# First layer of a graph network: normalizing the node rows in the edge stage instead of the perceptron stage

## The chip, the cores and the metric

The kernel runs on one core of one Trainium2 chip. The metric is the device time of the whole program in microseconds (us). Three runs of the kernel before took 6508.22, 6519.34 and 6523.56 us, so its median is 6519.34 us. Beside them there is one execution under the hardware profiler.

The engines are PE (TensorE, the matrix engine, with PEld for its weight loads), DVE (VectorE), ACT (ScalarE), POOL (GpSimd) and SP (SyncE, which issues plain DMAs here). POOL issues the indirect DMAs, gathers and scatters of rows.

## What is computed

Four layers over a graph of 50,000 nodes (padded to 50,176) and 25,000 edges (padded to 25,088), rows of 128 floats. Only the first layer is touched by the change:

```python
h = jnp.maximum(_layernorm(x, axis=-1), 0.0)
x = x + _L0_gnn_ref(h, edge_attr_128, W1, b1, W2, b2, gamma, beta, src, dst)

def _L0_gnn_ref(node_feats, edge_feats, W1, b1, W2, b2, gamma, beta, src, dst):
    msg = jax.nn.relu(node_feats[src] + edge_feats)
    agg = jax.ops.segment_sum(msg, dst, num_segments=n_nodes)
    h = node_feats + agg
    h = jax.nn.relu(h @ W1.T + b1) @ W2.T + b2
    mean = jnp.mean(h, axis=0)
    var = jnp.var(h, axis=0)
    return (h - mean) * jax.lax.rsqrt(var + BN_EPS) * gamma + beta
```

Layer normalization is over the 128 features of a row. The normalized rows h are needed in two places: for the 25,000 gathered source rows of the edges, and for all 50,000 nodes. The edges are sorted by destination.

## The kernel before

The program is a chain of stages (`prepare_indices`, `gine_edges`, `gine_mlp`, `gine_finish`, then two graph convolutions, an attention layer and a mean aggregation). A stage is a `Phase`: it allocates its tiles and semaphores, and at its end all engines meet at a barrier and POOL clears the stage's semaphores one by one (line 52). Inside a stage each engine has its own program, written out by hand; engines wait on semaphores. A tile is 512 rows: 128 partitions by 4 rows of 128 floats (`SUB` = 4), 256 KB.

`pipeline(eng, bodies, tiles, steps)` (line 228) writes an engine's order: for each turn t it emits every step (lag, function) for tile t - lag, in the order of the list. So the order of the list is the order of the engine's queue, and a step with lag 1 works on the tile before. A loop body holds 7 tiles in the edge stage (`K`) and 14 in the perceptron stage (`NB`), and each tile of a body has its own buffer, 7 of them (`RING`).

**The edge stage** (`gine_edges`, line 313) has 49 tiles of 512 edges, 7 bodies. SP loads the indices, the edge features and the `keep` row of each of the 7 tiles, then fills the table AGG in DRAM with zeros in 14 DMAs of 1792 KB (line 345), then reloads the tiles of the next body as their scatters land (`agg_out`). POOL (line 352) gathers the source rows of x with 4 indirect DMAs per tile (line 157), waits for the zero fill, and then, per body, scatters each tile's sums to AGG with 4 indirect DMAs (line 163); from the fourth tile on a gather of the next body follows each scatter, and the last four gathers of a body stand together. For each tile the other engines run a ring:

- DVE `moments`: statistics (line 186) and moments (line 194) of the gathered rows; ACT `root` (line 199); DVE `scales`: reciprocal (line 208) and shift (line 212); ACT `normalize`: four activations (line 217, the helper `Norm.apply`), which write relu((x - mean) / std) in place.
- DVE `add` (line 407) adds the edge features; PE `turn` transposes the message (line 420); ACT `copy_turned` (line 443) applies relu and copies it out of PSUM.
- DVE `scan` (line 400) sums along the sorted edges, with `keep` as the reset; PE `turn_back` (line 428) transposes back; ACT `copy_back` (line 448) writes `rows`, which POOL scatters.

DVE's list is moments, scan of the tile before, add (with the scales ahead of it). ACT's is root, copy_back of the tile before, normalize, copy_turned.

**The perceptron stage** (`gine_mlp`, line 455) has 98 tiles of 512 nodes. SP loads x and AGG of a tile; DVE takes the statistics of x, ACT the root, DVE reciprocal and shift, ACT normalizes x into `h` (four activations, line 217); POOL adds `agg` (line 511) and issues one small scatter to a table of positions POS (line 163); PE transposes (line 583), multiplies by W1 (line 590) and by W2 (line 596); ACT copies the transposed tile (`sT`, line 615) and makes the hidden layer (`hidT`, line 621); DVE adds the bias (line 538) and takes statistics for the batch normalization (line 543); SP stores YT. All of `gine_finish` reads YT and x and writes the DRAM tables X and H; H is written there for the first time.

## Time and profile before

| | |
|---|---|
| median of 3 runs | 6519.34 us |
| profiled execution, its own time | 6571.89 us |
| its span | 6570.1 us |
| busy, share of the span | PE 55%, PEld 31%, DVE 57%, ACT 39%, POOL 60% |
| granted TensorE clock, mean over the span | 0.767 |
| edge stage | from the barrier at about 29 us to POOL's last scatter, issued at 641.68 us |
| perceptron stage | from 652.7 us to about 993 us |

How to read the rows below. Times are us from the start of the span. In the table of stretches each row is a stretch, its length, the busy time of PE, PEld, DVE, ACT and POOL with the number of instructions in brackets, then the granted TensorE clock (1.00 is full), the busy share of the 16 DMA engines and GB/s. In the order of time each row is start, duration, engine, line, operation, what it writes <- what it reads, shapes, and x with the number of instructions merged into the row; in square brackets stands the time that the engine was idle before it and what released it. "issue" is time without a wait that the profile shows, "remote" a release that it ascribes to none of this core's engines. In the list of waits the columns are: who waited for whom, us in total, times, longest. SPq is SP's queue of DMA issues. A busy engine is not always at work: an instruction held by another one counts as busy.

### The profile page before, as it was taken

The page shows a single profiled execution, that of the slowest core. Times are in us where ns is not written, and L with a number is a line of the kernel's source. Part 1 is how long each engine was busy: PE and PEld are TensorE (multiplying, and loading weights), DVE is VectorE, ACT ScalarE, POOL GpSimd, SP SyncE. Part 2 cuts the span into 40 slices and gives each one's busy share as a digit, 9 for nine tenths or more (in the row PEclk, how much of TensorE's full clock was granted, in tenths as well). Part 3 has the DMA queues.
Part 4 walks back from the last instruction along what each step waited for, and adds up shares of the span by engine and source line. Part 5 has one row for each costly group of instructions (what it writes and reads, how often), then busy time and mean ns, then how long its engine had stood idle before and what let it go on. Part 6 is the DMA issues. An engine that isn't in the chain of part 4 may idle for free. (4 is left out here: it accounts for less than half of the span.)

```text
span 6570.1 us, 69946 instructions
## 1 busy us (share of the span) xinstructions
PE 3610.1 (55%) x13980; PEld 2028.2 (31%) x13980; DVE 3759.2 (57%) x11380; ACT 2554.3 (39%) x5795; POOL 3939.5 (60%) x3763
## 2 busy tenths in 40 slices
PE   1111673368775893454777689444223337995333
PEld 0111332222222453341322245343201115664222
DVE  2222898824345887992443588699635564554323
ACT  1222887724443114662444311577523332332000
POOL 4676667754451457885554145899866615554766
PEclk9999995578887997756898899656556668996555
DMA  7332769811111224541111022666445542333222
GB/s 231 84 87 64 258 227 337 307 42 35 36 37 29 65 67 153 175 152 45 39 40 35 24 72 70 208 233 235 151 125 178 173 142 65 104 103 111 85 79 69
DMA packets 507700, 784.36 MB, mean 119 GB/s; under 512 B 150737, under 2 KB 185144, under 8 KB 505568
## 3 DMA queue, kind: packets, MB, share of 16 engines
q1 hardware_dynamic: 413408, 623.08, 28.5%
q0 software_dynamic: 94080, 159.09, 8.9%
q14 instruction: 156, 1.28, 0.1%
q8 instruction: 56, 0.92, 0.1%
HBM read 476.20 MB, written 316.91 MB: 121 GB/s over the span
## 5 line engine op out<-in xcount | busy, mean ns | idle before, releaser
L913 DVE TENSOR_TENSOR conv_logits_leaky<-conv_logits_z,conv_logits_sloped 128x512 f32<-128x512 f32 x784 | 527.4, 689 | 538.3 <-ACT conv_logits_sloped L876 318.0
L157 POOL DMA_INDIRECT conv_logits_hd<-H,conv_logits_idx x392 | 370.7, 946 | 548.9 <-issue 448.1
L839 PE MATMUL conv_logits_z<-conv_logits_hdT,wsum 128*128 128x512 f32 x784 | 466.7, 733 | 277.8 <-issue 190.5
L876 ACT ACTIVATE conv_logits_sloped<-conv_logits_z 128x512 f32<-128x512 f32 x784 | 453.5, 601 | 401.4 <-remote 115.3
L1317 PE MATMUL conv_nodes_o_ps<-wmean,conv_nodes_hT 128*128 128x128 f32 x1568 | 338.6, 383 | 460.7 <-ACT conv_nodes_hT L1382 402.0
L163 POOL DMA_INDIRECT AGG<-conv_aggregate_rows,conv_aggregate_idx x392 | 381.7, 974 | 313.5 <-ACT conv_aggregate_rows L1159 178.2
L1317 PEld LDWEIGHTS conv_nodes_o_ps<-wmean,conv_nodes_hT 128*128 128x128 f32 x1568 | 289.8, 277 | 527.8 <-ACT conv_nodes_hT L1382 464.8
L157 POOL DMA_INDIRECT conv_logits_hs<-H,conv_logits_idx x392 | 370.7, 946 | 126.6 <-issue 126.6
L847 PE MATMUL conv_logits_z<-diffT,wl 128*128 (+1 forms) x784 | 385.8, 638 | 77.4 <-DVE conv_logits_leaky L913 77.4
L1123 PE MATMUL conv_aggregate_y<-wl,conv_aggregate_diff 128*128 128x512 f32 x784 | 408.3, 654 | 22.7 <-issue 14.3
L217 ACT ACTIVATE conv_nodes_scaled<-conv_nodes_o,conv_nodes_norm_shift,conv_nodes_norm_rstd 128x128 f32<-128x128 f32 x784 | 322.2, 481 | 169.0 <-DVE conv_nodes_norm_shift L212 164.7
L1186 DVE SCALAR_TENSOR_TENSOR conv_aggregate_part<-conv_aggregate_y,conv_aggregate_alpha,conv_aggregate_part 128x128 f32<-128x128 f32 x1176 | 358.4, 346 | 20.6
L839 PEld LDWEIGHTS conv_logits_z<-conv_logits_hdT,wsum 128*128 128x128 f32 x784 | 159.0, 222 | 573.9 <-issue 462.6
L1274 POOL TENSOR_TENSOR conv_nodes_agg<-conv_nodes_agg,conv_nodes_bias 128x512 f32<-128x512 f32 x196 | 248.5, 1268 | 105.8 <-DVE conv_nodes_res L1351 39.3
L157 POOL DMA_INDIRECT gat_aggregate_xd<-X,idx x196 | 185.4, 946 | 208.6 <-DVE gat_aggregate_x L1769 153.8
L903 DVE TENSOR_TENSOR diffT<-conv_logits_hsT_ps,conv_logits_hdT 128x512 f32 (+1 forms) x98 | 67.8, 692 | 397.2 <-ACT conv_logits_hdT L870 217.4
L163 POOL DMA_INDIRECT AGG<-gine_edges_rows,gine_edges_idx x196 | 203.2, 1037 | 151.4 <-issue 107.8
L1520 PE MATMUL gat_logits_e_ps<-gat_logits_hdT,gat_logits_wa 128*4 128x512 f32 x98 | 84.6, 963 | 375.5 <-ACT gat_logits_hdT L1533 176.1
L163 POOL DMA_INDIRECT out<-mean_edges_rows,idx x196 | 210.5, 1074 | 105.0 <-issue 57.3
L157 POOL DMA_INDIRECT gat_logits_hd<-H,idx x196 | 193.1, 985 | 127.7 <-remote 60.3
L1149 ACT ACTIVATE conv_aggregate_alpha<-conv_aggregate_alpha_ps 128x16 f32<-128x16 f32 x98 | 18.0, 184 | 566.2 <-issue 148.9
L157 POOL DMA_INDIRECT gine_edges_hs<-x,gine_edges_idx x196 | 199.1, 1016 | 61.4 <-issue 59.2
(249 smaller groups left out, 10371.5 us busy)
## 6 DMA issues: line engine op xcount, KB each, us to landing
conv_nodes_h<-H SPq DMA_DIRECT2D x196, 256.0 KB, 2.7
conv_nodes_agg<-AGG SPq DMA_DIRECT2D x196, 256.0 KB, 3.0
AGG<-gine_edges_zero SPq DMA_DIRECT2D x14, 1792.0 KB
gine_mlp_x<-x SPq DMA_DIRECT2D x98, 256.0 KB
gine_mlp_agg<-AGG SPq DMA_DIRECT2D x98, 256.0 KB
YT<-gine_mlp_yT SPq DMA_DIRECT2D x98, 256.0 KB
gine_finish_x<-x SPq DMA_DIRECT2D x98, 256.0 KB
gine_finish_yT<-YT SPq DMA_DIRECT2D x98, 256.0 KB
```

Source lines behind the costliest of these rows:

```text
L157: return pool.indirect_dma_start(out=out, out_offset=None, in_=table, in_offset=bass.IndirectOffsetOnAxis(ap=index, axis=0))
L163: return pool.indirect_dma_start(out=table, out_offset=bass.IndirectOffsetOnAxis(ap=index, axis=0), in_=rows, in_offset=None, bounds_check ...
L217: last = act.activation(out[:, a, :], x[:, a, :], func, bias=self.shift[k][:, a:a + 1], scale=self.rstd[k][:, a:a + 1])
L839: pe.matmul(z[h][:, :], g.wsum[:, h * D:(h + 1) * D], hdT[slot(k)][:, :], start=True, stop=True).then_inc(z_done[0], 1)
L847: pe.matmul(z[h][:, :], g.wl[:, h * D:(h + 1) * D], g.diffT[:, bass.ds(n * TILE, TILE)], start=False, stop=True, skip_group_check=True).th ...
L876: act.activation(sloped[H * j + h][:, :], z[h][:, :], ACT.Copy, scale=SLOPE).then_inc(sloped_made[j], 1)
L913: dve.tensor_tensor(leaky[H * j + h][:, :], z[h][:, :], sloped[H * j + h][:, :], ALU.max).then_inc(leaky_made[j], 1)
L1123: pe.matmul(y[s][:, :], diff[slot(k)][:, s * P:(s + 1) * P], g.wl[:, :], start=True, stop=True).then_inc(y_done, 1)
L1186: last = dve.scalar_tensor_tensor(out=out, in0=yh, scalar=a, in1=out, op0=ALU.mult, op1=ALU.add)
L1274: pool.tensor_tensor(flat(agg[r]), flat(agg[r]), bias[:, :], ALU.add).then_inc(agg_made, 1)
L1317: last = pe.matmul(o_ps[k % 2][:, a, :], hT[k % 2][:, a * P:(a + 1) * P], g.wmean[:, :], start=True, stop=True)
L1520: pe.matmul(e_ps[n % 2][:, :], wa[:, 1, :], hdT[n % 2][:, :], start=True, stop=False)
```

## The change

In the edge stage two tiles of nodes are now handled beside each tile of edges (49 x 2 = 98). SP loads their x rows and later stores the normalized rows to H; DVE and ACT do the normalizing, with steps of their own in their lists (`node_scales` and `node_normalize` one tile behind). The perceptron stage loads H in the place of x, has no normalizing left, and POOL's addition waits for the load itself. The lags of its lists shrink with the steps that are gone.

```diff
@@ gine_edges
+        x, h = ([m.sbs(f"{n}{c}_", [P, SUB, D]) for c in range(2)] for n in ("x", "h"))
+        node_norm = [Norm(m, f"node_norm{c}") for c in range(2)]
+        x_in, h_out = ([m.sems(f"{n}{c}_") for c in range(2)] for n in ("x_in", "h_out"))
+        node_made = [m.sem(f"node_made{c}") for c in range(2)]
...
+                def load_nodes(k, i):
+                    for c in range(2):
+                        sp.dma_start(x[c][k][:, :, :], node_rows(g.x, (i * K + k) * 2 + c)).then_inc(x_in[c][k], 16)
+                def store_nodes(k, i):
+                    for c in range(2):
+                        sp.wait_ge(node_made[c], i * K + k + 1)
+                        sp.dma_start(node_rows(g.H, (i * K + k) * 2 + c), h[c][k][:, :, :]).then_inc(h_out[c][k], 16)
                 for k in range(K):
                     load(k, 0)
+                for k in range(K):
+                    load_nodes(k, 0)
                 sp.wait_ge(zero_set, 1)
...
                         for k in range(K):
+                            store_nodes(k, i - 1)
+                            load_nodes(k, i)
                             sp.wait_ge(agg_out[k], i * 64 + agg0)
                             load(k, i)
+                for k in range(K):
+                    store_nodes(k, nb - 1)
...
+                def node_moments(k, i):
+                    for c in range(2):
+                        dve.wait_ge(x_in[c][k], i * 16 + 16)
+                        node_norm[c].take_stats(dve, x[c][k], k)
+                    for c in range(2):
+                        node_norm[c].moments(dve, k, i * K + k + 1)
+                def node_scales(k, i):
+                    for c in range(2):
+                        node_norm[c].invert(dve, k, i * K + k + 1)
+                    for c in range(2):
+                        node_norm[c].shifts(dve, k, i * K + k + 1)
-                pipeline(dve, nb, K, [(0, moments), (1, scan), (0, add)])
+                pipeline(dve, nb, K, [(0, moments), (1, scan), (1, node_scales), (0, node_moments), (0, add)])
...
+                def node_normalize(k, i):
+                    for c in range(2):
+                        act.wait_ge(node_norm[c].shift_done, i * K + k + 1)
+                        past(act, h_out[c][k], i * 16)
+                        node_norm[c].apply(act, h[c][k], x[c][k], k, ACT.Relu).then_inc(node_made[c], 1)
+                def node_root(k, i):
+                    for c in range(2):
+                        node_norm[c].root(act, k, i * K + k + 1, eps)
                 pipeline(act, nb, K, [
                     (0, lambda k, i: norm.root(act, k, i * K + k + 1, eps)),
-                    (1, copy_back), (0, normalize), (0, copy_turned)])
+                    (1, copy_back), (0, normalize), (1, node_normalize), (0, node_root), (0, copy_turned)])
@@ gine_mlp
-                    sp.dma_start(x[r][:, :, :], node_rows(g.x, n)).then_inc(tile_in[r], 16)
+                    sp.dma_start(h[r][:, :, :], node_rows(g.H, n)).then_inc(tile_in[r], 16)
...
-                node_stream(sp, nb, load, freed, store, 5)
+                node_stream(sp, nb, load, freed, store, 4)
...
-                    pool.wait_ge(h_made, n + 1)
+                    wait_alone(pool, tile_in[r], 32 * (turns(k, i) + 1), steps_own)
...
-                pipeline(dve, nb, NB, [
-                    (0, take_stats),
-                    (9, copy_y),
-                    (1, lambda k, i: norm.moments(dve, k % RING, i * NB + k + 1)),
-                    (3, lambda k, i: norm.scales(dve, k % RING, i * NB + k + 1)),
-                    (9, measure_y)])
+                pipeline(dve, nb, NB, [(6, copy_y), (6, measure_y)])
...
-                pipeline(act, nb, NB, [
-                    (0, lambda k, i: norm.root(act, k % RING, i * NB + k + 1, eps)),
-                    (2, normalize), (4, copy_turned), (6, hidden)])
+                pipeline(act, nb, NB, [(0, copy_turned), (2, hidden)])
```

Where the instructions stand now, at two places. First ACT in the loop of the edge stage, one tile, before (`norm_std` is the root, `rows` the copy back, `hs` the normalized gathered rows, `msgT` the copy of the turned message):

```order
L199 ACTIVATE gine_edges_norm_std<-gine_edges_norm_mv,gine_edges_eps 128x4 [waits gine_edges_norm_mv_done]
L448 ACTIVATE gine_edges_rows<-gine_edges_back 128x512 [waits scattered2,gine_edges_back_psum]
L217 ACTIVATE gine_edges_hs<-gine_edges_hs,gine_edges_norm_shift,gine_edges_norm_rstd 128x128 [waits gine_edges_norm_shift_done]
L217 ACTIVATE gine_edges_hs<-gine_edges_hs,gine_edges_norm_shift,gine_edges_norm_rstd 128x128 x3
L443 ACTIVATE gine_edges_msgT<-gine_edges_turned 128x512 [waits gine_edges_msgT_psum]
```

The same place after the change:

```order
L199 ACTIVATE gine_edges_norm_std<-gine_edges_norm_mv,gine_edges_eps 128x4 [waits gine_edges_norm_mv_done]
L483 ACTIVATE gine_edges_rows<-gine_edges_back 128x512 [waits scattered3,gine_edges_back_psum]
L217 ACTIVATE gine_edges_hs<-gine_edges_hs,gine_edges_norm_shift,gine_edges_norm_rstd 128x128 [waits gine_edges_norm_shift_done]
L217 ACTIVATE gine_edges_hs<-gine_edges_hs,gine_edges_norm_shift,gine_edges_norm_rstd 128x128 x3
L217 ACTIVATE gine_edges_h_3<-gine_edges_x_3,gine_edges_node_norm_shift,gine_edges_node_norm_rstd 128x128 [waits gine_edges_h_out0_3,gine_edges_node_norm0_shift_done]
L217 ACTIVATE gine_edges_h_3<-gine_edges_x_3,gine_edges_node_norm_shift,gine_edges_node_norm_rstd 128x128 x3
L217 ACTIVATE gine_edges_h_3<-gine_edges_x_3,gine_edges_node_norm_shift,gine_edges_node_norm_rstd 128x128 [waits gine_edges_h_out1_3,gine_edges_node_norm1_shift_done]
L217 ACTIVATE gine_edges_h_3<-gine_edges_x_3,gine_edges_node_norm_shift,gine_edges_node_norm_rstd 128x128 x3
L199 ACTIVATE gine_edges_node_norm_std<-gine_edges_node_norm_mv,gine_edges_eps 128x4 [waits gine_edges_node_norm0_mv_done]
L199 ACTIVATE gine_edges_node_norm_std<-gine_edges_node_norm_mv,gine_edges_eps 128x4 [waits gine_edges_node_norm1_mv_done]
L478 ACTIVATE gine_edges_msgT<-gine_edges_turned 128x512 [waits gine_edges_msgT_psum]
```

Eight activations and two roots now stand between the normalizing of a tile and the copy of its turned message. Second, DVE in the edge stage from the scan to the addition, after the change (before it, the reciprocal of the edge rows followed the scan at once):

```order
L422 SCALAR_TENSOR_TENSOR gine_edges_sumT<-gine_edges_keep,gine_edges_sumT,gine_edges_msgT 128x512 [waits gine_edges_scanned,gine_edges_msgT_made]
L208 RECIPROCAL gine_edges_node_norm_rstd<-gine_edges_node_norm_std 128x4 [waits gine_edges_node_norm0_std_done]
L208 RECIPROCAL gine_edges_node_norm_rstd<-gine_edges_node_norm_std 128x4 [waits gine_edges_node_norm1_std_done]
L212 SCALAR_TENSOR_TENSOR gine_edges_node_norm_shift<-gine_edges_node_norm_mv,gine_edges_node_norm_rstd 128x4 [waits gine_edges_node_norm0_rstd_done]
L212 SCALAR_TENSOR_TENSOR gine_edges_node_norm_shift<-gine_edges_node_norm_mv,gine_edges_node_norm_rstd 128x4 [waits gine_edges_node_norm1_rstd_done]
L186 BN_STATS gine_edges_node_norm_stats<-gine_edges_x_5 128x6 [waits gine_edges_x_in0_5]
L186 BN_STATS gine_edges_node_norm_stats<-gine_edges_x_5 128x6 x3
L186 BN_STATS gine_edges_node_norm_stats<-gine_edges_x_5 128x6 [waits gine_edges_x_in1_5]
L186 BN_STATS gine_edges_node_norm_stats<-gine_edges_x_5 128x6 x3
L194 BN_AGGR gine_edges_node_norm_mv<-gine_edges_node_norm_stats 128x2 [waits gine_edges_node_norm0_stats_done]
...
L208 RECIPROCAL gine_edges_norm_rstd<-gine_edges_norm_std 128x4 [waits gine_edges_norm_std_done]
L212 SCALAR_TENSOR_TENSOR gine_edges_norm_shift<-gine_edges_norm_mv,gine_edges_norm_rstd 128x4 [waits gine_edges_norm_rstd_done]
```

The scales of the last two node tiles and the statistics and moments of the next two stand ahead of the two small instructions that ACT's normalizing of the gathered rows waits for.

## Rows read from the trace of the kernel before

**Rows 1.** Table of stretches: the zero fill, the rest of the edge stage, the perceptron stage.

```profile
29.00:110.00 81.00, 14.46 (x52) 9.29 (x52) 24.44 (x86) 21.40 (x49) 28.16 (x29) 1.00 0.98 385
109.60:642.60 533.00, 94.75 (x340) 60.79 (x340) 142.88 (x505) 124.45 (x295) 374.40 (x364) 1.00 0.29 82
700.00:800.00 100.00, 76.97 (x256) 34.15 (x256) 98.94 (x379) 91.46 (x223) 71.35 (x64) 1.00 0.77 251
```

**Rows 2.** Order of time, edge stage: POOL's DMAs beside DVE's statistics and beside the scan.

```profile
256.59 0.95 POOL L157 DMA_INDIRECT gine_edges_hs<-x,gine_edges_idx  x1 [0.30 <-issue]
256.82 0.87 DVE L186 BATCH_NORM_STATS2 gine_edges_norm_stats<-gine_edges_hs 128x6 f32<-128x128 f32 x4 [5.10 <-issue]
306.05 1.36 POOL L163 DMA_INDIRECT AGG<-gine_edges_rows,gine_edges_idx  x1 [0.30 <-issue]
```

**Rows 3.** List of waits, 115 to 640 us.

```profile
ACT gine_edges_rows L448 <- remote: 89.8, 10, 10.5
ACT gine_edges_msgT L443 <- remote: 88.1, 11, 9.2
POOL AGG L163 <- ACT gine_edges_rows L448: 43.6, 7, 9.5
```

**Rows 4.** Order of time, edge stage: the ring of one tile, DVE and ACT.

```profile
302.81 0.69 DVE L407 TENSOR_TENSOR gine_edges_msg<-gine_edges_hs,gine_edges_ea 128x512 f32<-128x512 f32 x1 [9.79 <-ACT gine_edges_hs L217]
...
304.44 0.38 DVE L194 BATCH_NORM_AGGREGATE gine_edges_norm_mv<-gine_edges_norm_stats 128x2 f32<-128x6 f32 x4 [0.15 <-DVE gine_edges_norm_stats L186]
304.71 0.60 ACT L443 ACTIVATE gine_edges_msgT<-gine_edges_turned 128x512 f32<-128x512 f32 x1 [1.93 <-issue]
...
305.34 1.28 DVE L400 TENSOR_TENSOR_SCAN gine_edges_sumT<-gine_edges_keep,gine_edges_sumT,gine_edges_msgT 128x512 f32<-128x512 f32 x1 [0.53 <-issue]
306.54 0.15 DVE L208 RECIPROCAL gine_edges_norm_rstd<-gine_edges_norm_std 128x4 f32<-128x4 f32 x1
...
308.32 1.64 ACT L217 ACTIVATE gine_edges_hs<-gine_edges_hs,gine_edges_norm_shift,gine_edges_norm_rstd 128x128 f32<-128x128 f32 x4
...
309.99 0.69 DVE L407 TENSOR_TENSOR gine_edges_msg<-gine_edges_hs,gine_edges_ea 128x512 f32<-128x512 f32 x1 [3.10 <-ACT gine_edges_hs L217]
```

**Rows 5.** Order of time, edge stage: a shift and the scatter beside it.

```profile
149.45 0.97 POOL L163 DMA_INDIRECT AGG<-gine_edges_rows,gine_edges_idx  x1 [0.30 <-issue]
149.54 0.16 DVE L212 SCALAR_TENSOR_TENSOR gine_edges_norm_shift<-gine_edges_norm_mv,gine_edges_norm_rstd 128x4 f32<-128x4 f32 x1
```

**Rows 6.** Order of time, perceptron stage: the ring of one tile.

```profile
803.56 1.26 POOL L511 TENSOR_TENSOR gine_mlp_s<-gine_mlp_h,gine_mlp_agg 128x512 f32<-128x512 f32 x1 [0.78 <-ACT gine_mlp_h L217]
804.05 0.78 DVE L212 SCALAR_TENSOR_TENSOR gine_mlp_norm_shift<-gine_mlp_norm_mv,gine_mlp_norm_rstd 128x4 f32<-128x4 f32 x1
804.95 1.65 ACT L217 ACTIVATE gine_mlp_h<-gine_mlp_x,gine_mlp_norm_shift,gine_mlp_norm_rstd 128x128 f32<-128x128 f32 x4 [0.30 <-DVE gine_mlp_norm_shift L212]
806.50 0.57 ACT L615 ACTIVATE gine_mlp_sT<-gine_mlp_turned 128x512 f32<-128x512 f32 x1
806.74 1.26 POOL L511 TENSOR_TENSOR gine_mlp_s<-gine_mlp_h,gine_mlp_agg 128x512 f32<-128x512 f32 x1 [0.79 <-ACT gine_mlp_h L217]
```

**Rows 7.** Order of time: the second and the last of POOL's 98 additions.

```profile
677.70 1.27 POOL L511 TENSOR_TENSOR gine_mlp_s<-gine_mlp_h,gine_mlp_agg 128x512 f32<-128x512 f32 x1
...
976.49 1.27 POOL L511 TENSOR_TENSOR gine_mlp_s<-gine_mlp_h,gine_mlp_agg 128x512 f32<-128x512 f32 x1 [0.71 <-ACT gine_mlp_h L217]
```

**Rows 8.** Order of time: PE while the perceptron stage drains.

```profile
978.41 0.60 PE L583 MATMUL gine_mlp_turned<-gine_mlp_ident,gine_mlp_s 128*128 128x128 f32 x4
...
981.24 0.60 PE L583 MATMUL gine_mlp_turned<-gine_mlp_ident,gine_mlp_s 128*128 128x128 f32 x4
```

**Rows 9.** Order of time: POOL's first instruction after the barrier between the stages.

```profile
652.74 0.21 POOL L168 MEMSET gine_mlp_ident<- 128x128 f32 x1 [10.09 <-POOLq L52]
```

**Rows 10.** Order of time, edge stage: two neighbouring issues of SP in a late stretch.

```profile
366.22 0.70 SPq L339 DMA_DIRECT2D gine_edges_keep<-KEEP  x1
371.15 0.73 SPq L337 DMA_DIRECT2D gine_edges_idx<-IDX  x1
```

More of the change, by code:

```diff
@@ L464, in gine_mlp @@
         gamma, beta, eps = m.sb("gamma", [D, 1]), m.sb("beta", [D, 1]), m.sb("eps", [P, 1])
-        x, agg, h, s = (m.sbs(n, [P, SUB, D]) for n in ("x", "agg", "h", "s"))
+        agg, h, s = (m.sbs(n, [P, SUB, D]) for n in ("agg", "h", "s"))
         sT, hidT, yT = m.sbs("sT", [P, TILE]), m.sbs("hidT", [P, TILE]), m.sbs("yT", [P, TILE])
@@ L603, in _ @@
                 act.wait_ge(weights_in, 6 * 16)
-                def normalize(k, i):
-                    r, n = k % RING, i * NB + k
-                    act.wait_ge(norm.shift_done, n + 1)
-                    past(act, s_made, n + 1 - RING)
-                    norm.apply(act, h[r], x[r], r, ACT.Relu).then_inc(h_made, 1)
                 def copy_turned(k, i):
```

12 lines of the change are left out of this document (5 added, 7 removed).

## The prediction

> **What bounds the kernel now.** I read the table of stretches first, to find the two stages that the diff touches. The edge stage (29 to 643 us) has two parts. While AGG is filled with zeros the 16 DMA engines are busy 0.98 of the time at 385 GB/s, and no scatter may start [rows 1]. From 109.6 to 642.6 us it is a different picture: DMA 0.29, DVE 142.88 us and ACT 124.45 us of 533, and POOL 374.40 us in 364 indirect DMAs, 1.029 us each [rows 1]. Each of these has 0.30 us of issue ahead of it [rows 2], so POOL's queue wants 364 x 1.33 = 484 us; 49 us of idle time are left, 43.6 of them in 7 waits for the rows that ACT copies out [rows 3]. So **POOL's descriptor queue bounds the edge stage**, at 8 x 1.33 = 10.6 us a tile.
>
> Then the order of time, for the ring that feeds POOL: DVE adds, PE transposes ("turns"), ACT copies, DVE scans, PE turns back, ACT copies, ACT normalizes the next tile, DVE adds again. From add to add it takes 309.99 - 302.81 = 7.18 us [rows 4]. It has 3.4 us a tile to spare against POOL.
>
> In the perceptron stage DVE looks full (98.94 of 100 us) at a TensorE clock granted at 1.00, the 2.4 GHz level [rows 1]. It is not full of work: the shift of 128x4, 0.16 us elsewhere [rows 5], lasts 0.78 us and ends when POOL's addition ends [rows 6]. The ring is ACT's four normalizing activations (1.65 us), POOL's addition (1.26 us), DVE's shift, ACT again: 806.74 - 803.56 = 3.18 us [rows 6]. From the second addition to the last it is (976.49 - 677.70) / 96 = 3.11 us a tile [rows 7].
>
> **The change, part by part.**
>
> *Perceptron stage.* Statistics, roots, scales and normalizing go, 16 small instructions and their waits per tile. The loads stay two per tile (H in the place of x), so SP and DMA have what they had. POOL's addition waits for the load alone. What is late next: when the stage drains, ACT has no normalizing left and one tile takes 981.24 - 978.41 = 2.83 us, in the ring turn, copy, hidden copy, second product, turn [rows 8]. The order of these on PE and ACT is as before. That is the row I take. 96 tiles x (3.11 - 2.83) = **-27 us**. The bounds: nothing at all (0), or POOL's own pace. POOL's part of a tile is 1.26 + 0.16 + about 1.0 = 2.45 us, so (3.11 - 2.45) x 96 = -63. DMA is no bound: 3 x 262 KB a tile is 2.0 us at the 385 GB/s of the zero fill [rows 1]. The start is unchanged: after its first addition POOL waits for the store of POS.
>
> *Fourteen loads ahead of the zero fill.* They are 14 x 262 KB = 3.67 MB put into a queue that is the bound there; at 385 GB/s that is 9.5 us, and at the bandwidth of the fill's own part a little less. Everything from the first scatter moves by it: **+9 us** (bounds 0, if the loads slip into DMA's free beginnings, and 12).
>
> *The ring of the edge stage.* Per tile DVE gets 8 + 8 statistics instructions and 4 small ones, ACT 8 activations and 2 roots; POOL and PE get nothing. In the new order ACT does the node activations between normalize and the copy of the turned tile, and DVE does the node work between scan and add; both lie in the ring. From the end of normalize: 8 activations at 1.55 us per four, which is the distance from one group's start to the next instruction [rows 6], 3.1; two roots 0.5; copy to scan 0.63; scan to reciprocal 1.20; four small DVE instructions 0.7; statistics and moments of two tiles, each 0.87 and 0.38 [rows 2, 4] less 0.08 where one group starts into the other, 2 x 1.09 + 0.1 = 2.3; reciprocal, shift and hand-over 0.45; normalize and hand-over 1.67 [rows 4]. The sum is 10.5 us. The turns of PE and the copy back lie beside this. So the ring goes from 7.2 to 10.5 us and stands **level with POOL's 10.6**: in the middle of the stage it costs nothing, but the spare time is gone. It shows at the end, where POOL has only scatters left (4 x 1.33 = 5.3 us a tile) and the ring brings a tile each 10.5: two tiles late, 2 x 5.2 = **+10 us**. Bounds: 0, if the ring is still ahead by then; and if each added ACT instruction took its full busy time (8 x 0.48 + 2 x 0.29) with 0.3 more of waits, 11.4 us a tile, 49 x 0.8 = 39.
>
> *SP and DMA in the edge stage.* Four DMAs more per tile. SP waits for the node rows of tile k before it loads the next body's x, indices and edge rows of tile k; ACT makes these rows one tile behind, as it does the rows that the scatter waits for, so SP's wait for the scatter still comes last. 4 x 262 KB per 10.6 us are 99 GB/s beside 82 GB/s, far from 385. I take 0 (bounds 0 and 10). H's store waits only for itself, 7 tiles later.
>
> *Semaphores.* The edge stage clears 42 more and the next one 7 fewer. POOL's 10.09 us between the stages [rows 9] hold 34 clears beside a landing and a barrier, so 35 more are under 10; I take **+2**.
>
> *What VectorE's new work does to POOL.* A scatter beside the scan lasts 1.36 us instead of 0.97. A gather beside statistics lasts 0.95 and a scatter beside a 128x4 shift 0.97, nothing more [rows 2, 5]. So the added DVE work costs POOL 0. The Trainium skill, page SBUF — State Buffer, section on the two separate sides, says that a DVE instruction with two SBUF inputs and a GpSimd one that reads SBUF exclude each other through a shared port pair, for the whole instruction. The long scan agrees; by the rule the two added shifts of a tile would block too, 98 x 0.16 = 16 us more, and the sum would be 6529. The row of the shift speaks against it.
>
> The sum is -27 + 9 + 10 + 2 = **-6 us**, against the profiled execution (span 6570.1, itself 6571.9 us). That execution lies 52.6 us above the median 6519.34; I carry the difference over to the median, since no term scales with it: 6519 - 6 = **6513 us**.
>
> **The rivals.**
>
> *Rival 1, the ring passes its delays on (slower).* In some stretches ACT's copies start late although PE is done: 21 waits of 8.5 us in the mean, put down to no engine [rows 3], where about 2 us is normal [rows 4]. That is 21 x 6.5 = 137 us of delay, and 49 us of it reached POOL; the 3.4 us of spare time took the rest. Without spare time more reaches POOL. The copy of the turned tile is covered by 3.6 us of node work, so 2.9 of its 6.5 would show, 11 times: 32. The copy back shows about 5, 10 times: 50 to 65. With what lengthens the ring a little beyond POOL (0.3 a tile, 15), 97 to 112 in place of 49, so +48 to +63 on the sum; if only half the stretches come, +24. The middle of these ends is about +41, and with the sum's own -6 the time is 6519 + 35 = 6554. It decides from a ring longer than 10.6 us. Against it: the 52.6 us between the profiled execution and the median are as large as POOL's 49 us of idle time, so an execution without the profiler may hardly have these delays; then there is nothing to pass on.
>
> *Rival 2, all of the new work hides (faster).* The ring keeps ahead, the fill takes the loads for 3, and the perceptron stage goes at 2.7 instead of 2.83: -39 + 3 + 2 = -34, 6485. For it: DVE and ACT are idle for three quarters of the edge stage. Against it: PE and ACT keep their order, and the drained rows show it [rows 8].
>
> *Rival 3, SP falls behind.* SP issues 7 DMAs per tile instead of 3, in order, behind two new waits. In a late stretch two issues in a row stand 371.15 - 366.22 = 4.93 us apart [rows 10]; if all issues of one tile in three took half of that, 2.5, these tiles would need 17.5 us of SP against POOL's 10.6, and POOL would wait for its indices: 7 us on 16 tiles less what the lead of three tiles takes, some +90, 6603. Against it: SP now waits for scatters, not for its own issues.
>
> **How the numbers follow.** A measurement of this kernel tells 0.2%, 13 us, from no change: below 6506 is faster, above 6532 slower. The forecast has 0.47, with a range of its own of 6497 to 6527: it falls 0.12 faster, 0.32 same and 0.03 slower. Rival 1 has 0.33, of it 0.06 same and 0.27 slower. Rival 2 has 0.14, faster. Rival 3 has 0.06, slower. That makes 0.26 faster, 0.38 same, 0.36 slower. The range that leaves out the outer halves of rivals 2 and 3 and the tail of rival 1 is 6486 to 6575.
>
> **What would show it.** Right: the first scatter at about 118 us instead of 109.6; add to add in the edge stage 10 to 11 us everywhere, no longer 7.2; POOL's last scatter some 20 us later than 642; one perceptron tile in 2.83 us, and DVE half idle there, with no shift of 0.78 us left. Wrong: an add-to-add distance over 11.5 us, with POOL waiting for the copied rows for more than 70 us (rival 1); a perceptron tile still over 3 us or at 2.5; POOL waiting for its indices (rival 3); gathers longer than 1.0 us beside statistics.

## The result and the profile after

The changed kernel takes **6604.21 us** (median of 4 runs, 6591.32 to 6620.54), the kernel before 6520.73 us (4 runs, 6508.22 to 6523.56). The ratio is 1.0135, with a 95% interval of 1.0114 to 1.0155: slower by 83.5 us. The forecast was 6513 with a range up to 6575, and its likeliest case was wrong; the sign and the mechanism are those of rival 1, at about twice its price.

The profiled execution of the changed kernel took 6620.54 us (span 6618.7). First its table of stretches, zero fill, rest of the edge stage and 100 us of the perceptron stage, which answers to [rows 1]:

```profile
29.00:120.00 91.00, 13.35 (x48) 8.58 (x48) 40.99 (x222) 38.69 (x101) 27.12 (x29) 1.00 1.00 395
119.90:758.00 638.10, 95.82 (x344) 61.46 (x344) 254.14 (x1350) 276.46 (x734) 363.61 (x364) 1.00 0.46 141
810.00:910.00 100.00, 84.74 (x281) 37.37 (x280) 50.40 (x71) 41.11 (x71) 91.44 (x82) 1.00 0.88 282
```

POOL does the same 364 DMAs in 363.61 us, but the stretch is 638 us long in the place of 533. The perceptron stage is no longer full of DVE (50.40 for 98.94). Where the 105 us went is in the list of waits, 115 to 760 us, answering to [rows 3]:

```profile
ACT gine_edges_hs L217 <- DVE gine_edges_norm_shift L212: 183.3, 37, 17.0
POOL AGG L163 <- ACT gine_edges_rows L483: 149.7, 18, 13.9
...
DVE gine_edges_node_norm_mv L194 <- remote: 52.0, 19, 4.1
...
PE gine_edges_back L463 <- remote: 39.6, 5, 9.0
DVE gine_edges_norm_shift L212 <- remote: 28.9, 8, 8.2
ACT gine_edges_norm_std L199 <- remote: 27.6, 8, 7.0
DVE ne_edges_node_norm_shift L212 <- remote: 15.6, 6, 4.9
DVE gine_edges_norm_mv L194 <- remote: 12.5, 4, 5.6
```

POOL waits 149.7 us for copied rows, 106 more than before (43.6). The late releases ("remote"), before on ACT's two copies alone, now sit on DVE, PE and ACT's root, the new instructions among them. Order of time, edge stage; first two additions of an undisturbed part, then pieces of one tile in a late stretch:

```profile
314.96 0.69 DVE L429 TENSOR_TENSOR gine_edges_msg<-gine_edges_hs,gine_edges_ea 128x512 f32<-128x512 f32 x1 [1.72 <-ACT gine_edges_hs L217]
...
324.58 0.69 DVE L429 TENSOR_TENSOR gine_edges_msg<-gine_edges_hs,gine_edges_ea 128x512 f32<-128x512 f32 x1 [1.72 <-ACT gine_edges_hs L217]
```

```profile
207.72 0.69 DVE L429 TENSOR_TENSOR gine_edges_msg<-gine_edges_hs,gine_edges_ea 128x512 f32<-128x512 f32 x1 [2.89 <-ACT gine_edges_hs L217]
...
216.58 0.30 ACT L199 ACTIVATE gine_edges_norm_std<-gine_edges_norm_mv,gine_edges_eps 128x4 f32<-128x4 f32 x1 [4.95 <-issue]
...
219.39 0.16 DVE L212 SCALAR_TENSOR_TENSOR ne_edges_node_norm_shift<-gine_edges_node_norm_mv,ine_edges_node_norm_rstd 128x4 f32<-128x4 f32 x1 [5.93 <-issue]
...
234.48 1.65 ACT L217 ACTIVATE gine_edges_hs<-gine_edges_hs,gine_edges_norm_shift,gine_edges_norm_rstd 128x128 f32<-128x128 f32 x4 [14.74 <-DVE gine_edges_norm_shift L212]
...
236.16 0.69 DVE L429 TENSOR_TENSOR gine_edges_msg<-gine_edges_hs,gine_edges_ea 128x512 f32<-128x512 f32 x1 [1.71 <-ACT gine_edges_hs L217]
...
244.09 1.00 POOL L163 DMA_INDIRECT AGG<-gine_edges_rows,gine_edges_idx  x1 [13.43 <-ACT gine_edges_rows L483]
```

Undisturbed, a tile takes 9.62 us from add to add, 1 us less than POOL's 10.6 (in place of 7.18 in [rows 4]). The disturbed one takes 236.16 - 207.72 = 28.4 us: a root stands 4.95 us and a shift 5.93 us, both put down to "issue", and so on, each behind the other. POOL then stands 13.43 us.

At the end of the stage, where POOL only scatters, it waits for the ring at each of the last five tiles. The first of these waits lies behind a late stretch; the last four are 4.8 us each, 19.3 us together:

```profile
714.25 0.97 POOL L163 DMA_INDIRECT AGG<-gine_edges_rows,gine_edges_idx  x1 [13.87 <-ACT gine_edges_rows L483]
...
723.89 0.97 POOL L163 DMA_INDIRECT AGG<-gine_edges_rows,gine_edges_idx  x1 [4.84 <-ACT gine_edges_rows L483]
...
752.75 0.97 POOL L163 DMA_INDIRECT AGG<-gine_edges_rows,gine_edges_idx  x1 [4.82 <-ACT gine_edges_rows L483]
```

Two rows of the perceptron stage, 2.83 us apart (3.18 in [rows 6]), and the first instruction behind the barrier, answering to [rows 9]:

```profile
901.14 1.26 POOL L555 TENSOR_TENSOR gine_mlp_s<-gine_mlp_h,gine_mlp_agg 128x512 f32<-128x512 f32 x1 [0.33 <-issue]
...
903.97 1.26 POOL L555 TENSOR_TENSOR gine_mlp_s<-gine_mlp_h,gine_mlp_agg 128x512 f32<-128x512 f32 x1 [0.43 <-issue]
```

```profile
770.34 0.21 POOL L168 MEMSET gine_mlp_ident<- 128x128 f32 x1 [12.78 <-POOLq L52]
```

By stages, after less before: first scatter 119.97 for 109.59, +10.4; first to last scatter 636.6 for 532.1, **+104.5**; from there to the next stage +2.7; perceptron stage (from its identity fill to that of `gine_finish`) 316.7 for 344.1, **-27.4**. The sum is +90.2, and the medians without the profiler differ by 83.5. So the loss of the edge stage is no product of profiling. The two profiled executions as a whole differ by 48.6 us only: the rest of the program, which the change does not touch, took 5573 us in the one before and 5532 in this one. Most of the 52.6 us by which the profiled execution of the kernel before lay above its median would then stand behind the two stages; a second profiled execution of it, to compare with, there is not.

### The profile page after: what moved, and what is told of

It is laid out like the page before. It is cut to its first block and busy times, and to the rows that moved or that the text cites. A ratio compares the mean times of both kernels' runs of the same rounds, so it can differ in the third digit from the quotient of the medians.

```text
span 6618.7 us, 70480 instructions
## 1 busy us (share of the span) xinstructions
PE 3605.0 (54%) x13980; PEld 2023.8 (31%) x13980; DVE 3719.3 (56%) x11380; ACT 2556.7 (39%) x5795; POOL 3936.2 (59%) x3763
## 5 line engine op out<-in xcount | busy, mean ns | idle before, releaser
L163 POOL DMA_INDIRECT AGG<-gine_edges_rows,gine_edges_idx x196 | 196.1, 1000 | 259.7 <-ACT gine_edges_rows L483 149.7
L455 PE MATMUL gine_edges_turned<-gine_edges_ident,gine_edges_msg 128*128 128x128 f32 x196 | 54.6, 434 | 413.8 <-DVE gine_edges_msg L429 226.6
```

Source lines behind the costliest of these rows:

```text
L163: return pool.indirect_dma_start(out=table, out_offset=bass.IndirectOffsetOnAxis(ap=index, axis=0), in_=rows, in_offset=None, bounds_check ...
```

## The experiments

They ran on four chips, and the kernel before was timed beside each set: B 5732.1 us (e1 to e4), C 5731.9 (f1 to f4), D 6538 and 6540 (g1 to g3, h1 to h5), E 6497 (j1). So there are two kinds of chip for this kernel, the slower taking 13 to 14% more. The result's chip, A, is like D and E; its number was not noted, so it may be one of them. Each chip was used in one or two sittings, so what differs may also be something that goes along with the chip. This difference turned out to be the best experiment of the study. Ratios are to the kernel before on the same chip. The kernel before was traced on A alone, and the changed kernel was timed on A and C alone.

**The parts alone, chip B.** e1 has the new `gine_edges` with the old `gine_mlp`. e2 is the other way round:

```diff
 gine_mlp, e2 (gine_edges as before)
-   sp.dma_start(h[r][:, :, :], node_rows(g.H, n)).then_inc(tile_in[r], 16)
+   sp.dma_start(h[r][:, :, :], node_rows(g.x, n)).then_inc(tile_in[r], 16)
```

> Edge stage of the changed kernel, perceptron stage of the kernel before (it normalizes its rows itself; what the edge stage stored is overwritten later and read by nobody in between). Every theory in which the perceptron stage gained 27 us expects 6631 us (6604 + 27), 110 us over the kernel before. If the perceptron stage gained little without the profiler, the time is that of the changed kernel, 6604.

Measured: 5742.13 us, ratio **1.0016** (1.0006 to 1.0027). A miss for every theory: the edge part costs 9 us here and not 110. (By the traces the next stage begins 19.7 us later in e1 than in e2, 623.6 for 603.9; with no trace of the kernel before on this chip the 10 us between the two figures stay open.)

> Edge stage of the kernel before, perceptron stage of the changed kernel; it adds the plain node rows in place of the normalized ones, which leaves out the first normalization of the node rows. The traces give the perceptron stage 316.7 us for 344.1: 6493 us, 27 under the kernel before. It is the base that the two next runs are compared with. A gain under 10 us would say that the stage is bound by something else without the profiler.

Measured: 5694.19 us, **0.9937** (0.9923 to 0.9950), -36 us. By the traces of e1 and e2 the stage is 344.7 and 316.1 us long, -28.6; the 7 us between the two figures are open too.

e3 keeps the transfers and drops the work (its stores write one constant tile, so the normalization is left out); e4 keeps the work and drops the transfers (the perceptron stage adds plain rows):

```diff
 e3
-   sp.wait_ge(node_made[c], i * K + k + 1)
-   sp.dma_start(node_rows(g.H, ...), h[c][k][:, :, :])
+   sp.wait_ge(x_in[c][k], i * 16 + 16)
+   sp.dma_start(node_rows(g.H, ...), h[0][0][:, :, :])
-   (1, scan), (1, node_scales), (0, node_moments), (0, add)
+   (1, scan), (0, add)
-   (0, normalize), (1, node_normalize), (0, node_root), (0, copy_turned)
+   (0, normalize), (0, copy_turned)
 e4
-   store_nodes(k, i - 1)
-   load_nodes(k, i)
-   dve.wait_ge(x_in[c][k], i * 16 + 16)
+   dve.wait_ge(x_in[c][k], 16)
-   gine_mlp: node_rows(g.H, n)
+   gine_mlp: node_rows(g.x, n)
```

> The changed kernel without its work on the node rows in the edge stage: all loads of x and all stores into H are there, seven issues of SP to a tile, but VectorE and ScalarE do nothing with them (the stores write one constant tile, so the normalization is left out and the sums are of other numbers). Theory A, the work in the ring of an edge tile takes the spare time and lets delays through to POOL: 6493 + 9 (loads ahead of the zero fill) = 6502, 6495 to 6515. Theory B, the transfers and SP's issues in order slow the gathers and scatters: 6604 or nearly, at least 6570. Theory C, each is harmless alone and only the sum of them costs: under 6520 here and under 6520 in the next run.

Measured: 5722.10 us, 0.9984 (0.9975 to 0.9993).

> The changed kernel with its work on the node rows, but without the transfers: the fourteen tiles of x are loaded once and normalized again in every body, nothing is stored, and the perceptron stage adds plain node rows (so its output lacks the first normalization). Theory A: 6604 less at most 10, so 6590 to 6604, with POOL waiting some 150 us for copied rows as in the changed kernel. Theory B: about 6502. Theory C: under 6520.

Measured: 5700.30 us, 0.9944 (0.9930 to 0.9958). Both are under the kernel before, which is what theory C says, but nothing was there to be told apart: the whole loss was missing on this chip. The traces say why. No wait of the edge stage in e1 to e4 is put down to "remote", and POOL waits for copied rows for at most 1.2 us in each of the four.

**The changed kernel elsewhere, and delays by hand, chip C.** The delays, in the kernel before (f2) and in the changed one (f3):

```diff
 copy_turned
     act.wait_ge(msgT_psum, i * K + k + 1)
+    if k in (1, 3, 5):
+        for d in range(3):
+            past(act, pad_made, i * 9 + k // 2 * 3 + d)
+            act.activation(pad[:, :], zero[:, :], ACT.Copy).then_inc(pad_made, 1)
```

> The changed kernel itself, once more. Where the kernel before takes some 5730 us, as in the four runs above, the parts add up to 5732 + 9 (edge part, e1) - 38 (perceptron part, e2) = 5703, a ratio of 0.995, with POOL waiting under 5 us for copied rows in the edge stage. Where it takes some 6520 us, 1.0135 with 140 us of such waits. If the result of 1.0135 has a cause beside those waits, the ratio is over 1.000 here although they are missing.

Measured: 5712.41 us, ratio **0.9963** (0.9950 to 0.9977): the same program that loses 1.35% on chip A gains 0.4% here. Its table of stretches from the first scatter to the last, and DVE's additions (count, shortest, median and longest ns, first and last start):

```profile
119.00:607.00 488.00, 94.70 (x340) 60.73 (x340) 245.24 (x1349) 273.54 (x723) 376.70 (x364) 1.00 0.59 185
```

```profile
L429 DVE TENSOR_TENSOR gine_edges_msg<-gine_edges_hs,gine_edges_ea x42: 691/692/693, 154.9 to 590.3; 128x512 f32<-128x512 f32 x42
```

The stretch that took 638 us on chip A takes 488, with the same work and the same granted clock of 1.00, and the ring goes at POOL's pace: (590.3 - 154.9) / 41 = 10.6 us a tile.

> The kernel before with delays put in by hand: in tiles 1, 3 and 5 of each body of seven, ScalarE fills a buffer three times (estimate 9 us, from 597 ns for a 512 wide copy) between its wait for the turned messages and their copy, 21 delays in the stage. Theory A (a delay of the ring reaches POOL only as far as the tiles between have no spare time): the ring takes 7.2 us, POOL 10.6, so 2.33 tiles give back 7.9 us of each 9: 21 x 1.1 = 23 us over the kernel before, 10 to 60. Theory B (what a delay costs does not hang on the spare time, for the gathered tiles ahead absorb it or nothing does): 0, or 21 x 9 = 189 us.

Measured: 5760.38 us, 1.0057 (1.0043 to 1.0070), +28.5 us. One fill took 3.19 us, so a delay was 9.6 us. In the trace DVE's additions stand 7.2 to 7.5 us apart where there is no delay between them and 16.8 where there is one (9.5 to 9.8 and 19.2 in f3). POOL's waits for copied rows in f2, and behind them those of f3:

```profile
POOL AGG L163 <- ACT gine_edges_rows L454: 40.7, 11, 12.0
```

> The changed kernel with the same delays. Theory A: its ring takes 9.6 us, so 2.33 tiles give back 2.3 us of each 9: 21 x 6.7 = 141 us over the changed kernel, and some 90 us over the kernel before with the same delays (141 - 23 - 29), which would be the sign and the size of the result. Theory B: the same addition as in the kernel before.

Measured: 5840.83 us, 1.0196 (1.0182 to 1.0210), +128.4 us over f1 and **+80.5 over f2**.

```profile
POOL AGG L163 <- ACT gine_edges_rows L489: 141.9, 14, 14.4
```

21 delays by hand bring on this chip what chip A does by itself: 40.7 and 141.9 us of waits for 43.6 and 149.7, and 80 us between the kernels for 83.5. Number and length of the delays are near those of the late copies on A (21 of 8.5 us in the mean), so that the sizes agree is in part by design. What the two runs decide is that the same delays cost 28.5 us beside one ring and 128.4 beside the other: theory B, the same addition in both, falls.

f4 is f3 with one more edit, the edge tile's scales taken out of `add` into a step of their own:

```diff
-   (1, scan), (1, node_scales), (0, node_moments), (0, add)
+   (1, scan), (0, scales), (1, node_scales), (0, node_moments), (0, add)
```

> The changed kernel with the same delays and one edit: VectorE makes the scales of the edge tile right behind the scan, ahead of its work on the node rows, which then lies beside ScalarE's normalization of the edge tile. Theory A: the ring falls to some 8 us (7.18 and what ScalarE's 3.2 us of node rows stand over the 2.4 us of addition and turn), 2.33 tiles give back 6.0 of 9: 21 x 3 = 63 us over the changed kernel, some 78 us under the run before this one. If the order of the work does not matter (the busy time of the engines decides, which is the same), it is equal to the run before this one.

Measured: 5802.01 us, 1.0127 (1.0111 to 1.0142), 39 us under f3; the waits for copied rows are 95.9 us. The direction is right and the size half of the expected: the order decides, at equal busy times, but the ring takes 8.6 us from add to add where there is no delay, and not the 8 that I had reckoned.

**The same order without delays, chip D.** g1 is the changed kernel with f4's order. g2 also moves the fourteen first loads behind the zero fill and the node work three tiles back:

```diff
-   for k in range(K):
-       load_nodes(k, 0)
     sp.wait_ge(zero_set, 1)
...
+   for k in range(K):
+       load_nodes(k, 0)
-   DVE (1, node_scales), (0, node_moments)       ACT (1, node_normalize), (0, node_root)
+   DVE (4, node_scales), (3, node_moments)       ACT (4, node_normalize), (3, node_root)
```

> The changed kernel with VectorE's scales of the edge tile right behind the scan, no delays put in. Where the kernel before takes some 5730 us POOL is the bound in both and the time is the changed kernel's, ratio 0.996 (5705 to 5717). Where it takes some 6520 us, theory A gives 6604 less what the shorter ring takes up: with delays put in it was 39 us, so 6565, ratio 1.007; the theory that the ring's spare time does not decide there gives 6604.

Measured: 6580.45 us, ratio **1.0080** (1.0057 to 1.0104), as theory A has it (1.007); the 1.0135 that it is set against is from chip A. POOL's waits:

```profile
POOL AGG L163 <- ACT gine_edges_rows L485: 79.1, 13, 10.6
...
POOL gine_edges_hs L157 <- DMA gine_edges_idx<-IDX: 25.4, 4, 10.6
```

> The same with the fourteen first loads of x behind the zero fill, and with the work on the node rows three tiles later in the lists of VectorE and ScalarE, so that no edge tile waits for them. If the loads ahead of the zero fill cost the 9 to 10 us by which the first scatter moved, this kernel is 9 us under the one above, less what the three node tiles behind the last edge tile add at the end (3 x 3.2 us of ScalarE beside POOL's last scatters, 0 to 10 us): ratio to the kernel before 0.994 to 0.996. If the zero fill is not what the first scatter waits for, equal to the one above or slower by up to 10.

Measured: 6578.67 us, 1.0071 (1.0044 to 1.0098), no gain over g1 that can be told. Its first scatter starts at 109.1 us (118.6 in g1), so the loads ahead of the fill do cost 9.5 us there. The gain is lost at the other end: from the last scatter to the next stage it takes 23.2 us, 13.7 in g1, for the node rows now end three tiles behind (the last scatter is issued at 705.30 us, and ACT normalizes until 720.92). In between one wait took the place of another. POOL in the edge stage of g2 waits for nobody's rows, but 114.6 us for indices, where g1 has 79.1 and 25.4:

```profile
POOL gine_edges_hs L157 <- DMA gine_edges_idx<-IDX: 114.6, 19, 17.1
```

And SP's queue in a late stretch of it, where the x2 rows are two neighbouring issues:

```profile
311.53 0.70 SPq L341 DMA_DIRECT2D gine_edges_idx<-IDX  x1
315.04 0.70 SPq L342 DMA_DIRECT2D gine_edges_ea<-ea  x1
319.23 0.70 SPq L343 DMA_DIRECT2D gine_edges_keep<-KEEP  x1
325.53 4.90 SPq L352 DMA_DIRECT2D H<-gine_edges_h  x2
333.27 3.49 SPq L347 DMA_DIRECT2D gine_edges_x<-x  x2
337.50 0.31 SPq L341 DMA_DIRECT2D gine_edges_idx<-IDX  x1
338.01 0.38 SPq L342 DMA_DIRECT2D gine_edges_ea<-ea  x1
```

From one load of indices to the next SP takes 337.50 - 311.53 = 26 us; behind that it issues three loads in 1.1 us (the third, `keep`, at 338.57). This is rival 3, at work here, where the ring holds nothing up.

> The one above with the 21 delays put in. The node rows lie on the same places of the ring as in the run with the other order and delays (5802 us), so theory A gives that time less 0 to 9 us. If instead the first body profits (its seven tiles run without node work until the zero fill is through, and POOL does not wait for them), it is some 15 us under it.

Measured: 6687.16 us, 1.0229 (1.0198 to 1.0259), on chip D. The number to compare it with was from chip C, so the expectation can't be judged. Over g2, on the same chip, the delays cost 108.5 us.

**Work or transfers, on a chip that has the lateness (D).** h1 and h2 are e3 and e4 again.

> The kernel of e3 (loads of x and stores into H, no work of VectorE and ScalarE on the node rows; the normalization is left out) once more, for a chip on which the kernel before takes some 6520 us. Theory A (the work in the ring costs): before - 27 + 9, ratio 0.996 to 0.999, with some 44 us of waits of POOL for copied rows. Theory B (SP's seven issues a tile cost): 1.010 or more, with POOL waiting for indices. On a chip with the kernel before at 5730 us: 0.998 as in e3.

Measured: 6532.16 us, ratio **0.9991** (0.9967 to 1.0014). POOL and ACT:

```profile
ACT gine_edges_rows L485 <- remote: 77.1, 10, 10.5
POOL gine_edges_hs L157 <- DMA gine_edges_idx<-IDX: 52.8, 9, 10.1
```

> The kernel of e4 (the work on the node rows in the ring, no transfers for it in the loop; the perceptron stage adds plain rows) once more, for the same reason. Where the kernel before takes 6520 us theory A gives 1.011 to 1.0135 with some 130 to 150 us of waits of POOL for copied rows, theory B 0.996. Where it takes 5730 us: 0.994 as in e4.

Measured: 6645.25 us, ratio **1.0157** (1.0131 to 1.0182), somewhat over what I expected, and so are the waits for rows.

```profile
POOL AGG L163 <- ACT gine_edges_rows L476: 164.6, 20, 17.6
...
DVE ne_edges_node_norm_shift L212 <- remote: 32.0, 11, 6.3
```

The work in the ring brings a loss as large as that of the changed kernel, with SP at three loads a tile as before; the transfers alone bring little of it. SP's delays are there in h1: POOL waits 52.8 us for indices, and the 44 us of waits for rows that I expected are gone. One stands in the place of the other.

h4 lets POOL pause, in the changed kernel:

```diff
     for k in range(K):
...
+        if k in (2, 5):
+            wait_alone(pool, pad_made, i * 2 + k // 3, own)
+            pool.memset(pad[:, :], 0.0).then_inc(pad_made, 1)
         if more and k >= BEHIND:
```

> The changed kernel, with POOL filling a 128x3584 buffer (estimate 5.5 us, from 0.206 us for 128x128) before its gathers of tiles 2 and 5 of each body, so that it issues no transfer for that time, 14 times in all. If the late stretches end when POOL issues nothing for 5 us, the late waits in the trace (of PE, ScalarE, VectorE on engines that were done) fall to under a third of the changed kernel's 230 us, and the 77 us of fills are paid back by POOL's 150 us of waits for copied rows: ratio to the kernel before 1.000 to 1.010. If the pauses change nothing in them: the waits for rows still shrink by what the pauses cover, and the late waits stay, ratio 1.0135 to 1.020. Where the kernel before takes 5730 us, there are no late stretches and the pauses cost their own 77 us less POOL's spare: ratio 1.005 to 1.010.

Measured: 6619.68 us, 1.0126 (1.0099 to 1.0153). The late waits:

```profile
PE gine_edges_back L467 <- remote: 63.4, 9, 9.9
DVE ne_edges_node_norm_shift L212 <- remote: 51.4, 16, 6.7
ACT gine_edges_norm_std L199 <- remote: 44.4, 11, 6.5
DVE gine_edges_norm_shift L212 <- remote: 36.1, 9, 9.6
DVE gine_edges_node_norm_mv L194 <- remote: 33.4, 14, 4.0
DVE gine_edges_norm_mv L194 <- remote: 8.0, 2, 4.7
```

237 us, where the same sum over the changed kernel's list is 176 us (on chip A). They did not fall to a third. The time lies between the two forecast ranges and tells nothing by itself. But the fills were shorter than my estimate of 5.5 us:

```profile
L392 POOL MEMSET gine_edges_pad<- x14: 3108/3114/3127, 134.0 to 734.5; 128x3584 f32 x14
```

With pauses of 3.1 us the run doesn't answer what happens when POOL issues nothing for 5 us. The trace of the changed kernel has longer stops of POOL, nine of them of 10 us and more, and there the late stretches do end. It has 48 waits of 1 us and more put down to "remote" on DVE, ACT and PE; 12 of them end inside a stop of over 2.5 us, none later than 5.4 us after its beginning. Of SP's single issues of 0.7 us none starts later than 2.5 us into a stop, while 39 quick ones start later than 4 us into one. The stop of 13.43 us begins when the first of these transfers has ended, at 230.66:

```profile
229.72 0.94 POOL L157 DMA_INDIRECT gine_edges_hs<-x,gine_edges_idx  x1 [0.30 <-issue]
231.24 2.80 SPq L347 DMA_DIRECT2D gine_edges_x<-x  x2
234.08 0.33 SPq L341 DMA_DIRECT2D gine_edges_idx<-IDX  x1
```

So on a chip with late stretches they go along with POOL's issuing and end within some us of its stop. That the one makes the other is not shown: on B and C POOL issues as densely without them.

h5 is g2 with SP's `load(k, i)` ahead of `store_nodes(k, i - 1)` and `load_nodes(k, i)`.

> The kernel of g2 (other order, loads behind the zero fill, node rows three tiles later), with SP's loads for the edge tile ahead of its stores and loads of node rows in the loop. If POOL's 115 us of waits for indices in g2 came from SP standing at the wait for a node tile while the indices' turn had come, they fall to under 40 us and the time falls by some 75 us, to 6500, ratio 0.994 to 0.998. If they came from SP's slow issues as such, they stay over 80 us and the ratio is 1.005 or more. Where the kernel before takes 5730 us: 0.994 to 0.996, no waits for indices in either.

Measured: 6577.72 us, 1.0064 (1.0043 to 1.0085), no faster than g2.

```profile
POOL gine_edges_hs L157 <- DMA gine_edges_idx<-IDX: 71.7, 13, 8.3
POOL AGG L163 <- ACT gine_edges_rows L485: 44.5, 5, 10.3
```

The waits for indices fell by 43 us and 44.5 us of waits for rows came in their place. Neither theory had this: part of the 114.6 us was SP's order, part its slow issues, and what one wait gives up the next one takes.

**The perceptron gain without the edge work, chip E.** j1 is the kernel before with these lags:

```diff
-   (2, normalize), (4, copy_turned), (6, hidden)        (9, copy_y) (9, measure_y)      store, 5
+   (3, normalize), (5, copy_turned), (7, hidden)        (10, copy_y) (10, measure_y)    store, 6
```

> The kernel before with one step more between the scales of a tile and its normalization in the perceptron stage (ScalarE's three steps, VectorE's two last and the store moved by one tile), nothing else. A tile takes 3.18 us there, of which ScalarE works 2.9 and waits 0.30 for the shift that POOL's addition holds up. If that wait is what keeps the stage from POOL's pace, it takes 2.9 to 3.0 us a tile: 98 x 0.2 = 20 us less, ratio 0.996 to 0.998 on either chip. If VectorE is the bound, held by POOL's additions whatever the order, nothing changes (0.999 to 1.001).

Measured: 6484.44 us for 6496.87, ratio **0.9983** (0.9967 to 1.0000). The stage takes 334.3 us in its trace for 344.1 on A, -10, half of what I gave it. ACT no longer waits for the shift; POOL still waits for ACT:

```profile
L217 ACT ACTIVATE gine_mlp_h<-gine_mlp_x,gine_mlp_norm_shift,gine_mlp_norm_rstd 128x128 f32<-128x128 f32 x331 | 135.3, 480 | 0.0
L511 POOL TENSOR_TENSOR gine_mlp_s<-gine_mlp_h,gine_mlp_agg 128x512 f32<-128x512 f32 x83 | 104.8, 1262 | 51.5 <-ACT gine_mlp_h L217 46.2 <-issue 5.3
```

From 700 to 800 us ACT is busy for 94.29 of 100 us, 91.46 before, so ACT's own work is then the bound, or nearly. It is the only version with the whole computation that lies below the kernel before on a chip of the slow kind, and its interval reaches 1.0000. It was not run on the fast kind, where the changed kernel itself has 0.9963.

## Why the prediction was wrong

**The perceptron stage, -27: right.** -27.4 by stages on chip A, -28.6 on B, one tile in 2.83 us as in the drained rows.

**Fourteen loads ahead of the zero fill, +9: right.** +10.4 on A; g2 took 9.5 of it back at the first scatter.

**Semaphores, +2: right**, 2.7 us.

**SP and DMA, 0: nearly right for the time, wrong as a description.** h1 bounds the transfers with the loads ahead of the fill: 0.9991 less the gain of the perceptron stage, taken from A and B, leaves +21 us on D, of which about 10 are the fill's. The other 11 lie at my upper bound. SP does fall behind in the late stretches: POOL waits 52.8 us for indices in h1 and 21.2 in the changed kernel, 2.2 before.

**VectorE's new work costs POOL nothing: right.** Scatters last 1048 ns in f1 for 1036 in e2, 196 x 0.012 = 2.4 us in all. The Trainium skill, page SBUF — State Buffer, section on the two separate sides, has a DVE instruction with two SBUF inputs and a GpSimd one that reads SBUF exclude each other. By my estimate from that rule the 98 added shifts were worth 16 us, and the runs show under 3 us for the whole of the added work. In f1 no DMA that has a shift beside it, and no scan or addition, lasts over 1.00 us, while those beside a scan last up to 1.90, so the page's rule fits the scan and not the shift.

**The ring, +10 at the end of the stage: this is the step that failed.** The term had "in the middle of the stage it costs nothing" and +10 at the end; from the first scatter to the last the runs showed +104.5 us, with 149.7 us of waits for copied rows in place of 43.6. It holds two errors. The small one: the ring is 9.62 us and not 10.5. What it costs at the end depends on whether it is ahead by then. In f1 POOL's last 28 scatters follow each other without a wait, from 568.96 to 605.56 us; on chip A the ring is behind and the end costs 19.3 us, the mechanism of my +10 at twice its size. The large error is the sentence that carried the choice between the forecast and rival 1: "an execution without the profiler may hardly have these delays". I had seen the 21 late copies [rows 3], and took the 52.6 us between the profiled execution and the median for their absence, because POOL's idle time had the same size. That was a coincidence. The medians differ by 83.5 us and the profiled executions' stages by 90; the lateness is there without the profiler, and it comes with the chip. In the middle of the stage the ring's spare time had been worth some 100 us, and I had priced its loss at nothing.

**Rival 1 had the mechanism and half its price, and its condition was wrong.** It was to decide only from a ring longer than 10.6 us, and the ring of 9.62 lets the delays through. It gave 97 to 112 us of waits reaching POOL in place of 49; there were 149.7. With f2 and f3 the account is plain: 21 delays of 9.6 us are 201 us; the old ring has 3.4 us of spare time on 49 tiles, 167, and the new one 1.0, 48. So 34 and 153 us should reach POOL, and 40.7 and 141.9 did. On chip A the same reckoning is loose. The lateness beyond the normal was 137 us before; against 167 us of spare time nothing should have come through, and 44 did, so the lateness is not spread evenly over the tiles. 137 - 48 = 89, and with these 44, 133 for the 149.7: an estimate made afterwards, which no run tests. I had made discounts instead, for the cover of the turned copy and for a mean over half the stretches. What I had also missed is that the added instructions come late themselves (the shift at 219.39 us, 5.93 us behind the one before it on DVE); in h2 they do so with no added transfer.

Of the list of what would show it: the first scatter, the perceptron tile and the missing 0.78 us shifts came nearly as said. POOL's last scatter came 115 us later and not 20. Of the sign set for rival 1 the half with POOL came, more than 70 us of waits for copied rows; the add-to-add distance is over 11.5 us in the disturbed tiles and 9.62 in the others. POOL's waits for its indices, the sign of rival 3, came too, but short.

What stays open: what makes chips A, D and E late. It is not the added transfers: the lateness is in [rows 3] and [rows 10] before any change. POOL's issuing has a part in it by the trace, but h4, which was to settle that, paused too shortly. That it costs the rest of the program too was not followed up; behind the perceptron stage the traces have 5532 and 5573 us on A and 4774 to 4777 on B. The edge stage and the perceptron stage together account for the result on chip A; on the other chips the kernel before was not traced. I tried no version that is faster on both kinds by more than a measurement can tell.

## What to carry to other kernels

The spare time of a ring beside the engine that bounds a stage is a buffer against lateness, and work placed into it is free only if nothing comes late. Before calling such work hidden, sum the late waits in the trace, divide by the tiles and compare with the spare time that remains: on chip A late waits of 2.8 us a tile before the change let 44 us through against 3.4 of spare time, and 150 came through when 1.0 was left. A difference between a profiled execution and the median is evidence for nothing until it is found in a stage; and where a kernel gains on one chip and loses on another, put delays in by hand on the quiet chip, which shows the mechanism without its disturbance.

## What the runs showed of the hardware that I had not expected

- The same program takes 5732 us on chips B and C and 6497 to 6540 on A, D and E, with the same granted clock of 1.00 in the edge stage. From the first scatter to the last the edge stage of the kernel before takes 483.6 us on B (in e2) and 532.1 on A, with POOL's DMAs equally long (373.95 and 374.40 us for 364 of them in their stretches).
- On the slower chips there are stretches in which PE, ACT, DVE and SP all start late. SP's issues of 0.31 to 0.38 us become 0.70 us and stand 3.5 to 4.2 us apart; POOL's DMAs stay at 0.97 us with 0.30 us between them. In the changed kernel, of the waits of 1 us and more that are put down to "remote", none ends later than 5.4 us after POOL has stopped issuing, in stops of up to 13.9 us.
- An indirect DMA beside bn_stats (0.95 us) or beside a 128x4 shift (0.94 to 1.00 us in f1) is not lengthened; one beside the 128x512 scan lasts up to 1.90 us there. Over the stage, doubling and more of DVE's busy time (142.76 us in e2, 245.24 in f1) added under 3 us to POOL's busy time (373.95 and 376.70).
